# Moving the first context loads ahead of a wait, and two bias loads between two loads of x

## The reference, cut to what matters

```python
x = x + xattn(layernorm(x), ctx, ctx, Wq, bq, Wk, bk, Wv, bv, gamma, beta)   # cross attention, 32 pairs of 64 rows
x = x + attn(layernorm(x), w_kv, w_q, b_q, w_out, b_out)                     # low-rank self attention over 32 latents
x = x + ffn(layernorm(x), router_w, ..., sh_gate, sh_up, sh_down)            # 16 experts, top 2, and a shared one

def xattn(query, key_in, value, ...):
    q = query @ Wq + bq
    k = key_in @ Wk + bk
    v = value @ Wv + bv
    result = softmax(q @ k.T) @ v
    y = result + query
    return normalised(y) * gamma + beta
```

## Time and profile before

| what | us |
|---|---|
| median of 3 runs | 528.17 (527.53 to 528.89) |
| the profiled execution | 528.1 |
| its span, first to last instruction | 525.9 |
| around the span | 2.2 |
| TensorE busy | 494.0 (94% of the span) |
| VectorE / ScalarE / GpSimd busy | 387.0 / 219.0 / 203.5 |

### The profile page before, as it was taken

How to read it: one execution, slowest core, us unless ns; L and a number is a source line. 1 busy time by engine, 2 the same in 40 slices (tenths; PEclk the granted TensorE clock), 3 DMA queues, 4 the chain that set the end, 5 groups by cost and what they waited for, 6 DMA issues and landing times.

```text
span 525.9 us, 14488 instructions
## 1 busy us (share of the span) xinstructions
PE 494.0 (94%) x5028; PEld 347.1 (66%) x5029; DVE 387.0 (74%) x1053; ACT 219.0 (42%) x656; POOL 203.5 (39%) x344
## 2 busy tenths in 40 slices
PE   7999999999999999999999999999989879999990
PEld 7776665665666666666665667766745658888870
DVE  4788899998888788998552688888776315555764
ACT  3254433345344243444431466756431025555520
POOL 5000422212222221122222576775776605666640
PEclk9999999999999999999999999999999979999996
DMA  8979997986988799884115999710122235555747
GB/s 286 376 266 362 232 287 253 325 289 200 290 273 280 280 308 300 293 279 124 31 41 172 269 302 297 217 52 1 53 80 82 90 101 151 161 157 145 236 104 237
DMA packets 67611, 108.93 MB, mean 207 GB/s; under 512 B 8371, under 2 KB 49381, under 8 KB 67560
## 3 DMA queue, kind: packets, MB, share of 16 engines
q1 hardware_dynamic: 60872, 97.57, 59.1%
q0 software_dynamic: 3792, 8.43, 4.6%
q10 hardware_dynamic: 2896, 2.23, 1.5%
HBM read 85.31 MB, written 24.85 MB: 209 GB/s over the span
## 4 chain that ended last, share of the span: by engine, by line
PE 81%; POOL 5%; DVE 4%; DMA 4%; issue 3%; ACT 1%; SPq 0%; POOLq 0%; DVEq 0%
PE banks L1200 18%; PE banks L1226 18%; PE banks L1611 8%; POOL rows_by_expert L780 4%; PE banks L1214 4%; PE banks L1623 4%; PE banks L1239 3%; PE banks L1153 2%; PE banks L1605 2%; PE banks L1338 2%; PE banks L1390 2%; PE banks L1247 2%; PE banks L1345 2%; PE banks L1361 1%; PE banks L1169 1%
## 5 line engine op out<-in xcount | busy, mean ns | idle before, releaser
L1735 DVE STREAM_TRANSPOSE ctxT<-ring 128x832 f32<-128x832 f32 x124 | 118.2, 1009 | 1.4 <-DMA ring<-in_ctx_dram 1.1
L1200 PE MATMUL banks<-ctxT,qT_all 32*64 32x416 f32 (+2 forms) x2048 | 94.8, 498 | 1.1 <-issue 1.1
L1226 PE MATMUL banks<-ring,prob 128*64 128x256 f32 (+1 forms) x832 | 93.6, 381 | 0.7 <-ACT prob L897 0.7
L1226 PEld LDWEIGHTS banks<-ring,prob 128*64 128x64 f32 (+1 forms) x832 | 58.6, 137 | 31.5 <-issue 4.2
L1200 PEld LDWEIGHTS banks<-ctxT,qT_all 32*64 32x64 f32 x2048 | 56.3, 131 | 30.7 <-issue 13.3
L679 POOL TENSOR_TENSOR var<-mv,eps 128x1 f32<-128x1 f32 x32 | 6.1, 191 | 149.7 <-DVE mv L1776 95.6
L814 POOL DMA_INDIRECT expert_out<-prob,dest x47 | 46.2, 984 | 41.1 <-issue 21.7
L1611 PE MATMUL banks<-ring,ctxT 128*128 x188 | 50.4, 392 | 0.1
L910 ACT ACTIVATE prob<-banks,negmax 128x416 f32<-128x416 f32 (+2 forms) x80 | 41.0, 532 | 22.4 <-DVE negmax L1757 18.5
L1747 DVE TENSOR_REDUCE blockmax<-banks 128x1 f32<-128x416 f32 (+1 forms) x64 | 32.3, 566 | 19.2 <-PE banks L1200 19.2
L727 POOL TENSOR_TENSOR ctxT<-ctxT,k_mask 128x1088 f32<-128x1088 f32 x16 | 33.1, 2069 | 24.9 <-ACT ctxT L1011 24.9
(11 more groups left out here) (279 smaller groups left out, 947.6 us busy)
## 6 DMA issues: line engine op xcount, KB each, us to landing
ring<-in_ctx_dram SPq DMA_DIRECT2D x48, 1024.0 KB, 8.7
qT_all<-q_by_pair SPq DMA_DIRECT2D x56, 128.0 KB, 8.1
rows_by_expert<-blank SPq DMA_DIRECT2D x8, 774.0 KB, 5.7
ctxT<-rows_by_expert SPq DMA_DIRECT2D x47, 129.0 KB
mid<-stage SPq DMA_DIRECT2D x30, 128.0 KB, 2.3
ring<-in_ctx_dram SPq DMA_DIRECT2D x16, 130.0 KB
ctxT<-mid SPq DMA_DIRECT2D x16, 128.0 KB, 3.6
qT_all<-mid SPq DMA_DIRECT2D x16, 128.0 KB, 4.2
```

Source lines behind the costliest of these rows:

```text
L1200: last = pe.matmul(S[a][64 * b:64 * b + 64, 0:KW[a]], q_rep[mine, r, c, 64 * b:64 * b + 64], ctxT[mine, c, b, 0:KW[a]], start=c == 0, stop ...
L1226: last = pe.matmul(U[64 * b:64 * b + 64, 0:D], probT[0:rows, k, 64 * b:64 * b + 64], ring[0:rows, r, b, k, :], start=k == 0, stop=k == KT)
L1735: dve.transpose(ctxT[:, c].rearrange("p b (k j) -> p (b k) j", j=Q), ring[:, r].rearrange("p b k c -> p (b k) c")[:, :, columns(c):columns ...
```

## The change

The three large parts of pair 0 and then `load_x(2)` are issued before SyncE waits for the zeroed tails; only the tail part stays behind the wait. So `load_x(2)` now also goes ahead of the tail part. On ScalarE's queue the order becomes x0, bq, bk, x1 in place of x0, x1, bq, bk. Nothing else changes, and no instruction is added or removed.

```diff
@@ sync @@
+            for g in range(len(KPARTS) - 1):
+                load_part(0, 0, g, ctx_first if g < 2 else None)
+            load_x(2)
             sp.wait_ge(tails_ready, RING)
-            for g in range(len(KPARTS)):
-                load_part(0, 0, g, ctx_first if g < 2 else None)
+            load_part(0, 0, len(KPARTS) - 1)
             sp.sem_inc(ctx_loaded[0], 32)
-            load_x(2)
             load(1, 1)
@@ scalar @@
-            for n in range(2):
+            def load_x(n):
                 part = slice(*XPARTS[n])
                 act.dma_start(x_all[:, part, :], x_rows[:, part, :]).then_inc(x_loaded[n], 16)
+
+            load_x(0)
             act.dma_start(bq_col[:, :], t["L0_xattn_bq"].rearrange("(k p) -> p k", p=P),
                           allow_slow_non_contiguous=True).then_inc(qkb_loaded, 16)
             act.dma_start(bk_col[:, :], t["L0_xattn_bk"].rearrange("(k p) -> p k", p=P),
                           allow_slow_non_contiguous=True).then_inc(qkb_loaded, 16)
+            load_x(1)
             act.wait_ge(wT_done, 1)
```

## The result

| | before | after |
|---|---|---|
| median | 528.53 (527.53 to 530.16) | 537.36 (536.34 to 538.11) |
| ratio, 95% interval | | 1.0187 (1.0158 to 1.0215) |
| profiled execution / span | 528.1 / 525.9 | 538.11 / 535.9 |
| mean granted clock | 0.985 | 0.974 |

The kernel became 8.8 us slower by the medians, and 10.0 us by the two profiled executions. The forecast was 530.1 in a range of 528.2 to 532.0: the sign was right, and the size was off by a factor of more than four.

What follows compares the result with a forecast made beforehand. TensorE, busy 494.0 of 525.9 us, was taken as the bound. Sooner context 0, tail behind x 0, sooner biases 0 and later x1 +2.0 us on 528.1 gave 530.1, range 528.2 to 532.0.

Steps and rivals of the forecast that it cites:

- D = L - 8.5: TensorE's start: each us that x1 lands (L) after 8.5 us delays TensorE (D) by one; 2.0 us forecast.
- The landing of x1: ScalarE's queue: x1, now last, lands at 10.5 us instead of 6.2, between 9.6 and 11.4.
- the turns: DMA engines: queues served one packet each in turn, so x1 pays 16 turns against context packets, 3.1 to 3.6 us.
- bk's place: Last place in ScalarE's queue, where bk landed at 10.8 us; x1 would land then, its bytes balancing near 0.
- Rival (d): DMA queues: turns cost more for 1 KB packets or biases meet context fully, 531.1 to 532.1; 0.17 together with Rival (c).
- Part 1: SyncE's queue: context issued ahead of the wait, at most 0.45 us sooner; taken as 0 at the kernel's end.
- The tail part: SyncE's queue: tail behind load_x(2) costs 0 to 0.2 us by itself, 0 when covered by x1's delay.
- The clock: TensorE's clock after its early holes: no cost in the sum; a drop was only a rival, up to 3.4 us more.
- Rival (c): TensorE's clock drops after holes at the start, up to 3.4 us more, 531.5 to 533.5; 0.17 together with Rival (d).
- The page's rule on packets: DMA engines drain typically 9 to 17 descriptors from one queue before switching; x1 would pass in one or two turns.
- Faster: TensorE's start moved by sooner context or biases, at most 0.5 us, 527.6; measuring faster had chance 0.03.
- the rival (a): ScalarE's queue: x1 slips through in time, landing at 7.5 to 8.5 us, 528.1, partly so up to 529.5; chance 0.27.

Runs made afterwards that it cites:

- the 1 KB kernel: The changed kernel with pair 0's first two context parts fetched as eight transfers of 1 KB rows, not two of 4 KB rows; ratio 1.0106 (1.0062 to 1.0150).

## Why the prediction was wrong, point by point

- **What bounds the kernel; the slack of x1.** Right, and to a tenth. The rule D = L - 8.5 gives 5.05 for L = 13.55, measured 5.02; 3.9 for the ScalarE half's 12.4, measured 3.87; 2.8 for 11.3 with one bias ahead, measured 2.75. That nothing gives a late start back held in the main: 1.3 us came back in the scores of pair 0, and in the kernel with the context alone some 2 us more by its end.
- **The landing of x1 was the first mis-sized term:** 10.5 taken (the middle between 9.6 and 11.4, and not nearer to the row of bk, as it says), upper end 11.4, measured 13.55. Of its parts, the turns were right: 16 turns of 1 KB against 4 KB were put at 3.1 to 3.6 us and took 3.3 (bk at 10.3, x1 at 13.55). Wrong was the step that x1 lands in "bk's place" at 10.8 with the bytes in balance, together with the one that the biases get through sooner, by 5.8 at best. Both took the 331 packets of ScalarE's queue from 5 to 6 us as given. Somewhat over 100 of these were rows of x1, and the rest tiny; with the order turned round the queue passed 122 there in the changed kernel (beside 67 of q1), and 121 with the context at its old place (beside 22). By 6 us it had passed 752 of its 1088 packets before, 616 with the new order alone, and 531 with both halves. The missing 136 and 221 had to take turns with context packets instead. An estimate from these counts and the 205 ns of a turn gives 136 / 16 x 0.205 = 1.7 us and 2.8 us on top of 10.8, so 12.5 and 13.6; measured were 12.4 and 13.55. So of the 3.05 us by which L was missed, 1.15 came with the sooner context, and 1.9 are there with the new order alone. Why the tiny packets did not pass faster in that microsecond stays open. Rival (d) described this, but at 0.17 together with the clock, and with L to 12.5 only.
- **Part 1 at 0** was wrong too. I looked for who waits for the context and found nobody; the price was at those whom the context makes wait. bk's slack is 12.0 - 10.8 = 1.2 us, and this half alone moved bk by 2.7. The tail part held: VectorE's eight half transposes ran without a break in the changed kernel, and also with the context alone, where they began at 15.73.
- **The clock was the second mis-sized term.** The sum put it at nothing, and it cost 5.1 us. Rival (c) had the mechanism, at up to 3.4 us and against it that the holes would be short. With the true landing the hole is 4.6 us, and the lower level lasted 13 to 14 us instead of the 6.90 of the earlier trace rows. And the argument against it, that the holes are short with work between them, did not bear either: the clock fell after a hole of 1.62 us in the kernel with the context alone, and after holes of 1.31 and 0.69 us in the one with the new order and the later context. (c) and (d) are not independent of the forecast either: a later landing makes a longer hole, so their costs add, and the upper end of the range had to hold the sum.
- **The page's rule on packets** ("DMA: Bandwidth & Descriptors" of the Trainium skill, "Queues, rings and completion order"), several descriptors of one queue in a row, does not fit. The 92 packets of one queue beside 94 of the other in the microsecond from 7 us would not decide it, since equal bursts give equal counts, and the prediction's argument from the spread of bk was too weak for the same reason. The order of the packets decides it: 165 of 165 from 9.5 to 11.5 us stood singly between packets of the other queue.
- **Faster** (0.03) did not come, and the rival (a), x1 in time, had 0.27 on the strength of the same stretch of rows. It is what happens when the context is held back (x1 at 6.3).

## What to carry to other kernels

A DMA issued sooner has a price even when nobody waits longer for it: look at what is still in flight on the other queue, in how many packets, and how long the new neighbour's packets are. A small transfer of one element per packet belongs ahead of large-packet traffic or away from it, and what TensorE needs first does not belong behind it. A rate read in one stretch of a trace holds for the packets that were in it, and need not hold when their order is changed. Where a late transfer would open a hole in TensorE's work, price the lower clock after the hole on top of the delay, from the start and not as a separate case.

## What the runs showed of the hardware

- Holes in TensorE's work at the start and the stretch at the 1.2 GHz level that followed, one traced execution each: after 1.62 us, and after the pair of 1.31 and 0.69, about 6.9 us; after the pair of 2.44 and 0.69, and after 3.17, some 10 us; after 4.6 and after 5.3, more than 13. In the 1 KB kernel the pair of 0.86 and 0.69 us kept the full level. With the hole of 4.6 us filled the level stayed up too.
- Where both queues had packets, the engines took them singly in turn (changed kernel, 9.5 to 11.5 us). Beside context packets of 4 KB (159 ns each) 16 turns cost 2.7 us for element-sized packets and 3.3 us for rows of 1 KB. The landings agree: with the context issued at 1.9 or 2.3 us, bk came 2.7 to 3.3 us after the transfer ahead of it, and x1, where last, 3.3 us after bk.
- How fast element-sized packets pass when little else is there is not settled. In the kernel where the context waits for x1, 462 packets of ScalarE's queue, nearly all of them element-sized, passed in one microsecond beside 232 rows of Wk. With the ScalarE half alone, 121 passed from 5 to 6 us beside 22 packets of q1, at 20 GB/s in all. The cause of this slow microsecond is open.
- A transfer is there when the last of its engines has brought its share, and that one can be far behind: half had brought x1 by 8.4 us and the last one at 11.03, in the kernel with the new order and the later context.
- The hole in TensorE's work at 23.74 us, put down to issue, is missing in the changed kernel, and this gives 1.3 us back. It is missing too in the kernel with the old order and the later context, whose time is that of the kernel before, and it is there, at 0.10 to 1.10 us, in six others. What opens it was not tried, so the 1.3 us may not belong to the change.
